# Moving the addition of two gated products from VectorE to GpSimd in five of six groups of an attention ring

## What is computed

```
ss, sd = sigmoid(x @ Ws), sigmoid(x @ Wd)          # (b, t, 8 heads, 5 experts)
ss_g, sd_g = ss * top3(ss), sd * top3(sd)          # three of five experts kept
q5 = (x @ Wq).reshape(b, t, H, E, DH)              # H=8, E=5, DH=64
q = einsum('bthed,bthe->bhtd', q5, sd_g)           # gated sum over the experts; k and v alike, with ss_g
attn = softmax(q * DH**-0.5 @ k^T)
out = attn @ v
y[t, m] = sum over h, e of (out[t, h] @ Wo[e]) * top3(sd)[t, h, e]
```

## Time and profile before

| | us |
|---|---|
| median of three runs | 712.01 |
| the profiled execution, its own time | 711.09 |
| span of the profiled execution, first to last instruction | 709.3 |
| the loop of three turns: first gated product of turn 1 to that of turn 2 | 164.47 to 222.78 |
| the same, turn 2 to turn 3 | 222.78 to 283.71 |
| PE busy, whole span | 580.5 (82%) |
| DVE busy | 507.1 (71%) |
| ACT busy | 346.4 (49%) |
| POOL busy | 376.5 (53%) |

### The profile page before, as it was taken

The page is one execution under the profiler, slowest core; times in us unless marked ns, Lnnn a source line. Parts: engine busy times, 40 slices in busy tenths (PEclk is TensorE's granted clock), DMA queues, the critical chain, the costliest instruction groups (busy, mean ns, idle before and its releaser), DMA issues. The chain is left out here.

```text
span 709.3 us, 15705 instructions
## 1 busy us (share of the span) xinstructions
PE 580.5 (82%) x5739; PEld 391.0 (55%) x5739; DVE 507.1 (71%) x1069; ACT 346.4 (49%) x750; POOL 376.5 (53%) x340
## 2 busy tenths in 40 slices
PE   5399865769868859976747879999999999888897
PEld 5277622245344425434643446777677677666795
DVE  4936899967974982995885677776776767577653
ACT  2333300044243243425722668877877887625554
POOL 5514345663763755667447556666866665732221
PEclk9999997858968985996656999999999999999998
DMA  6311000020000000000220000000000000000000
GB/s 186 109 43 30 31 30 0 0 90 1 2 0 1 0 0 0 0 0 0 61 61 30 2 1 2 2 1 3 2 2 2 2 2 2 2 1 1 2 14 22
DMA packets 14175, 13.12 MB, mean 18 GB/s; under 512 B 3120, under 2 KB 11936, under 8 KB 14112
## 3 DMA queue, kind: packets, MB, share of 16 engines
q1 hardware_dynamic: 14112, 12.25, 5.9%
HBM read 11.72 MB, written 0.52 MB: 17 GB/s over the span
## 5 line engine op out<-in xcount | busy, mean ns | idle before, releaser
L1468 POOL TENSOR_TENSOR attn<-work,attn 128x512 f16<-128x512 f32 (+1 forms) x96 | 141.9, 1480 | 85.7 <-ACT attn L1275 85.7
L807 DVE TENSOR_TENSOR work<-banks,gatev 128x512 f32<-128x512 f32 x120 | 79.0, 682 | 17.0 <-PE banks L513 16.5
L1368 DVE TENSOR_REDUCE nmax<-banks 128x2 bf16<-128x1024 f32 x64 | 77.8, 1216 | 2.8 <-PE banks L1120 1.7
L511 PE MATMUL banks<-weights,xbTh 128*128 128x512 f16 x120 | 50.2, 418 | 28.4 <-DVE work L807 26.3
L1272 ACT ACTIVATE work<-banks,maskbias 128x512 f32<-128x512 f32 x64 | 44.2, 691 | 41.1 <-PE banks L1146 41.1
L2056 PE MATMUL banks<-ident,work 128*128 128x128 f32 x276 | 51.8, 325 | 8.6 <-DVE work L2256 3.0
L942 POOL TENSOR_TENSOR work<-work 128x512 f32<-128x512 f32 x24 | 30.4, 1268 | 43.9 <-DVE work L807 41.7
L1164 PE MATMUL banks<-work,attn 128*128 128x65 f16 x512 | 51.9, 196 | 1.6 <-POOL attn L1468 1.0
L1164 PEld LDWEIGHTS banks<-work,attn 128*128 128x128 f16 x512 | 48.3, 100 | 8.0 <-POOL attn L1468 4.5
L1165 PE MATMUL banks<-work,attn 128*128 128x65 f16 x512 | 52.0, 196 | 0.0
L1166 PE MATMUL banks<-work,attn 128*128 128x65 f16 x512 | 51.9, 196 | 0.0
(11 more groups left out here) (328 smaller groups left out, 1874.7 us busy)
## 6 DMA issues: line engine op xcount, KB each, us to landing
stage<-in_L_ffn_w SPq DMA_DIRECT2D x8, 512.0 KB, 4.0
stage<-in_L_ffn_Wkv SPq DMA_DIRECT2D x4, 640.0 KB, 4.1
stage<-in_L_ffn_Wq SPq DMA_DIRECT2D x2, 640.0 KB, 4.6
xt<-in_x SPq DMA_DIRECT2D x1, 512.0 KB, 4.4
ct<-in_ctx SPq DMA_DIRECT2D x1, 512.0 KB, 5.6
wo<-in_L_xattn_Wo SPq DMA_DIRECT2D x1, 512.0 KB
stage<-in_L_xattn_Wv SPq DMA_DIRECT2D x1, 512.0 KB, 3.6
stage<-in_L_xattn_Wq SPq DMA_DIRECT2D x1, 512.0 KB, 3.5
```

The lines of the kernel that those rows point to most:

```text
L511: pe.matmul(o, xh, wh, start=True, stop=False)
L807: dve.tensor_tensor(heads8(m.prod[:, k, e, :]), heads8(bank_pj[c % 2][:, :]), wide(g, DH1), ALU.mult).then_inc(s.prod_ready, 1)
L1368: dve.tensor_reduce(m.nmax[:, p % 2, i, :], banks[:, 6:8, :], AX.X, ALU.max, negate=True).then_inc(s.c_max_done, 1)
L1468: pool.tensor_tensor(m.Pl[:, p % 2, kts, :], m.Pf[:, kts, :], m.Ph[:, p % 2, kts, :], ALU.subtract).then_inc(s.c_P_lo, 1)
```

## The change

In the loop, for groups 0 to 4, the pair addition on DVE is left out, and POOL adds product 3 and product 4 itself, one after the other. Group 5 of each turn, and all six groups of batch 0, stay as they were.

```diff
-DVE_STEPS_B, POOL_STEPS_B, DVE_STEPS_C = 4, 16, 8
+DVE_STEPS_B, POOL_STEPS_B, DVE_STEPS_C = 4, 21, 8
...
+        def pair_on_dve(b, k):
+
+            return isinstance(b, int) or k == SUMS - 1
...
-                if e == E1 - 1:
+                if e == E1 - 1 and pair_on_dve(b, c // E1):
                     dve.wait_ge(s.prod_ready, b * X1 + (c + 1))
                     dve.tensor_tensor(m.prod[:, k, 3, :], m.prod[:, k, 3, :], m.prod[:, k, 4, :], ALU.add).then_inc(s.pair_ready, 1)
...
-                pool.wait_ge(s.pair_ready, b * SUMS + (k + 1))
-                pool.tensor_tensor(acc, acc, pr[:, 3, :], ALU.add).then_inc(s.acc_ready, 1)
+                if pair_on_dve(b, k):
+                    pool.wait_ge(s.pair_ready, SUMS if isinstance(b, int) and k == SUMS - 1 else b + SUMS if k == SUMS - 1 else k + 1)
+                    pool.tensor_tensor(acc, acc, pr[:, 3, :], ALU.add).then_inc(s.acc_ready, 1)
+                else:
+                    pool.wait_ge(s.prod_ready, b * X1 + (k * E1 + 4))
+                    ch.link(pool.tensor_tensor(acc, acc, pr[:, 3, :], ALU.add))
+                    pool.wait_ge(s.prod_ready, b * X1 + (k * E1 + 5))
+                    pool.tensor_tensor(acc, acc, pr[:, 4, :], ALU.add).then_inc(s.acc_ready, 1)
                 pool.wait_ge(s.acc_ready, b * SUMS + (k + 1))
                 pool.sem_inc(s.prod_free, 1)
```

## The result

| | before | after |
|---|---|---|
| median, nine runs each, us | 712.67 (707.45 to 714.02) | 716.2 (713.26 to 719.08) |
| ratio | | 1.0054, interval 1.0032 to 1.0075 |
| span of the profiled execution, us | 709.3 | 714.3 |

The change makes the kernel about half a percent slower: inside the 1% that was called no change, and clear of zero. The range held 716.2; the forecast of 712.6 was 3.6 us too low.

What follows compares the result with a forecast made beforehand. A turn hangs on when POOL starts summing z, how long that takes, and DVE's first row maximum. Terms 0, 0.4 and 0.1 make 0.5 us a turn; 3 x 0.5 = 1.5 on 711.09 gives 712.6, range 706 to 718.

Steps and rivals of the forecast that it cites:

- POOL's chain: POOL's additions, groups 0 to 4: 5.88 us a group without pause, from a second addition of group 0 that does not move.
- DVE's gain: DVE up to group 5's first product: of 3.6 us saved a turn, 2.2 left after waiting for group 3's ring slot.
- The pair addition of group 5: Group 5's pair addition on DVE falls among POOL's back-to-back additions: 0.1 to 0.3 us later end of group 4.
- The race: After group 4, DVE wakes in 0.2 us and starts its first masked copy before POOL's next addition at 0.32 us.
- The slower rival: DVE wakes later than 0.32 us, POOL's addition goes first, all three copies held: 714.6 to 719.7 us; chance 0.29.
- The alternation: Masked copies and POOL's group 5 additions take turns at SBUF; first row maximum at 200.45, before 200.47: 0 us a turn.
- z's end: Both splits of v fall between POOL's sums of z and hold POOL up twice: z ends 0.4 us later a turn.
- The late row maxima: Third row maximum slips from 204.67 to about 208.1; PE's 1.77 us idle covers it: 0.1 us a turn, bounds 0 or 1.6.
- The faster rival: Masked copies run through beside POOL's additions, the port does not bind: 1.75 us a turn faster, 705.9 us; chance 0.15.

Runs made afterwards that it cites:

- e10: Kernel before, with six added DVE reductions of a PSUM bank behind the splits of v each turn, result unused: 717.31 us, ratio 1.0084.
- e3: Changed kernel, with loop splits of v and masked copies of tile 0 reading one operand from PSUM (values not the reference's): 709.34 us, ratio 0.9940.
- e2: Changed kernel, with the loop's masked copies of tile 0 reading one operand from PSUM (values not the reference's): 710.0 us, ratio 0.9957.
- e7: Kernel before, with the first row maximum of a turn made ahead of the masked copies: 710.89 us, ratio 0.9992.
- e1: Changed kernel, with the loop's splits of v reading one operand from PSUM (values not the reference's): 713.15 us, ratio 1.0010.

## Why the prediction was right or wrong

**POOL's chain** was right. 5.88 us a group against 5.87; no pauses. Only its start in turn 1, said not to move, came 0.66 us later (169.19).

**DVE's gain** was right in its size at the end of the stretch, not in its cause. DVE's first product of group 5 came at 191.40 - 169.19 = 22.2 us behind POOL's second addition, 1.9 us earlier than before (192.64 - 168.53 = 24.1), where 2.2 were forecast. The wait for the ring slot that the prediction named isn't there: DVE has no idle time ahead of that product. Between the second addition and that product DVE's busy time fell by 3.0 us, not 3.6 (one pair addition in a row of instructions takes 0.61, not 0.72), and its idle time rose by 1.1, of it 0.6 in waits for TensorE's banks and 0.5 for ACT's high halves. So TensorE and ACT become part of the bound.

**The pair addition of group 5** was mis-sized: 0.1 to 0.3 us were put on group 4's end; POOL's addition took 1.80 instead of 1.27, 0.53 us.

**The race** went as forecast: copy 1 starts 0.22 us after group 4's end (0.2 taken), 0.1 us ahead of POOL's next addition, in all three turns. The slower rival's mechanism did not occur, though the time came out among its values; that the range held owes something to the room that was left for this rival. (Its far end, 711.1 + 3 x (1.4 + 1.6), is 720.1 and not 719.7.)

**The alternation** of copies and additions was right: 1.75 and 1.74 us for copies 2 and 3, and POOL's additions held beside them. The row maximum came 32.29 us after the second addition of group 0, "as before" in the forecast; 31.96 was before. These 0.33 us are nearly the mis-sized collision.

**z's end** was forecast 0.4 us later; measured 0.66: 0.3 in the sums (6.63 us for the first tile instead of 6.33), as forecast, and 0.34 at their start, from the term above.

**The late row maxima** are the step that failed. The third was forecast 3.4 us late and came 3.76 us late, but 0.1 us a turn was put on it, since TensorE's idle 1.77 us was to cover it, with a bound of 1.6 us. That idle time is of turn 1, at 2.4 GHz, and the cover held there: in turn 1 of the changed kernel TensorE still waits 0.87 us for z, and nothing shows through. "Three turns behave alike" is what was wrong, and the table ahead of the prediction had turns of 58.31 and 60.93 us: in turn 2 of the kernel before, at 1.2 GHz, TensorE has no idle time ahead of z's transposes. In turns 2 and 3 of the changed kernel, at that clock, it comes 1.2 us late. With 3 x 0.66 = 2.0 and 0 + 1.2 + 1.2 = 2.4 in place of 3 x 0.5 the sum would have come to 711.09 + 2.0 + 2.4 = 715.5, against 716.0 of the profiled execution, in which one turn more runs at the lower clock there (1.2 us). e10, where the maxima are late and z is in time, costs (717.31 - 712.3) / 3 = 1.7 us a turn by its median.

**The faster rival** (the port does not bind) names the right condition: e3 is that case for the copies and the splits, at 709.3, where 705.9 was forecast for it.

*Open:* whether late maxima make turns at the lower clock more frequent. The two are not tied to each other: turns 1 and 2 of e10 and turns 2 and 3 of e2 and e7 have late maxima at 1.00, and turn 2 of the kernel before has them in time at 0.50. But the changed kernel has two such turns of three and the one before has one, each in a single profiled execution, and no run held the clock fixed.

## What to carry to other kernels

Work moved between VectorE and GpSimd is not priced by durations alone: list the VectorE instructions with two SBUF operands that will run while GpSimd is at work, and count for each the rest of GpSimd's instruction; an operand from PSUM, or a GpSimd that is idle at that time, makes it free. Move as much as GpSimd makes up before VectorE's next such instruction (here two groups of six: 0.5% faster; three or four: no difference; five: 0.5% slower). And follow every instruction that gets late to its second consumer: here the row maxima feed a chain of their own, which joins the first one in TensorE's order. Idle time that is to cover a delay has to be read in every turn of a loop, at the clock that was granted there, and not in one.

## What the runs showed of the hardware

Held instructions take turns: with both engines queuing, a VectorE instruction of 0.68 us took 1.75 and a GpSimd addition of 1.27 took 1.51 to 1.72, and in the stretch shown neither engine ran two in a row while the other waited. That one PSUM operand frees a `tensor_tensor` from this altogether was seen in e1 and e2 (0.68 us, all nine copies and six splits). The same collision can fall on either engine: in e2 the pair addition of group 5 took 1.79 us in turn 1, held by the addition that in the changed kernel was held by it. TensorE's way from z to the addition into `x` took 2.5 us at a granted clock of 1.00 and 3.7 at 0.50 where TensorE was on time; the three transposes of z took 0.55 and 0.90 us.
